# The preparation of the last attention: x in quarters, normalised on ScalarE, one half rope table, first weights split there

## The chip, the core and the metric

The kernel runs on one core of a Trainium2 chip. The metric is the device time of one execution in microseconds. A core has TensorE (PE), VectorE (DVE), ScalarE (ACT), GpSimd (POOL) and the queue of SyncE (SP), which issues all the DMAs here. The engines run beside each other and wait for each other only at semaphores.

## The reference

Four blocks follow each other on x of 32 x 64 tokens by 512, each a gated cross attention and a gated feed-forward part; every part works on the layer norm of x. The change lies ahead of the last cross attention (32 heads of 128 in 8 groups, rotary positions, 64 tokens in a sequence), cut here to what matters:

```python
x = x + tanh(g_xattn[3]) * _L3_xattn_ref(_layernorm(x), ctx, ctx, pos, mask, Wq, Wk, Wv, Wo)

q = (query @ Wq).reshape(nb, q_len, H, D).transpose(0, 2, 1, 3)
cos, sin = cos_t[position_ids][:, None], sin_t[position_ids][:, None]   # tables of 512 positions
q = q * cos + _rotate_half(q) * sin                                     # k likewise
scores = jnp.where(mask == 0, -1e9, q @ k.T / sqrt(D))
x = softmax(scores) @ v @ Wo
```

A position below zero counts from the end of the table, and positions are cut to the table's ends.

## The kernel before

The 2048 tokens are 16 tiles of 128, handled in 4 turns of 4 tiles (QUAD, TURNS). The kernel is four stages; a stage ends when all engines are done, then POOL clears each of the stage's semaphores, one by one, and all engines meet (`stage`, lines 62 to 70).

1. `prepare_weights` loads and splits the weights of the early layers into a bfloat16 high half and a low half (raw minus high). SP issues the loads in an order written out by hand; the last things are the 4 MB of Wk3 and Wv3, whose split is stored to DRAM for later.
2. `early_layers` does everything up to the last attention in four turns and stores x to DRAM (`x_mid`); it also makes all keys and values of the last attention (`k3`, `v3`).
3. `prepare_last` loads the whole x (4 MB), the positions broadcast to 128 partitions, two tables (cos and sin, [512, 128] each), the mask and the first group's Wq and Wo. VectorE turns the positions to f32, wraps and clamps them (lines 1601 to 1607, on 2048 columns). Then four turns. In a turn VectorE makes bn_stats and bn_aggr of four tiles, POOL the reciprocal root (add, power, one column at a time, lines 1560 to 1563), VectorE the normalised tile (L1626). TensorE multiplies each table with the one-hot of the turn's 512 positions (L1574; four matmuls a table, two passes each in f32) and transposes the tiles (L1581); ScalarE copies cos, sin and the high halves of the transposed tiles (L1590, L1593), VectorE their low halves (L1632). VectorE makes the one-hot of turn t + 1 (L1615) before the low halves of turn t. The mask (L1642) comes last.
4. `last_attention` runs over 8 groups (its "heads"). Before the first one ScalarE and POOL split the loaded Wq into four pieces (L1973, L2084) and Wo into four (L2001, L2098). TensorE projects the first queries (L349 to L351) piece by piece, VectorE multiplies by cos and sin (L2141 to L2143), POOL adds the two (L2079). In POOL's program the four low halves of Wo stand behind the seven first rotations and ahead of the first division by the softmax's sum (L2092). SP reloads Wo and Wq for the second group once these low halves are made.

PSUM banks are handed on by counting semaphores (`Banks`): `wait_free` waits for the last drain of a bank, `wait_filled` for its matmuls. POOL opens them with one increment for each semaphore at a stage's start.

Of the kernel before, what the change touches and what calls it, by code (L numbers as in the profile page):

```python
# [21 lines left out]
F32 = mybir.dt.float32  # L22
# [7 lines left out]
P = 128  # L30
# [44 lines left out]
def prepare_weights(nc, io, w):  # L75

    with ExitStack() as ctx:
# [16 lines left out]
        eight = sb("eight", [P, E01])  # L94
# [14 lines left out]
        def _(sp):  # L109
# [97 lines left out]
        def _(dve):  # L207
            dve.memset(w["L1W"][:, 0:3, :], 0.0).then_inc(zeroed, 1)
            dve.memset(w["heads"][:, :], 0.0).then_inc(zeroed, 1)
            for k, name in enumerate(RAW):  # L210
                dve.wait_ge(raw_high, k + 1)
                dve.tensor_tensor(w[name + "l"][:, :, :], raw[name][:, :, :], w[name + "h"][:, :, :], ALU.subtract)
# [1292 lines left out]
def prepare_last(nc, io, w):  # L1505
# [3 lines left out]
    for j in range(QUAD):  # L1509
        plan.append((("turn", j), j))  # L1510
    plan += [(("cos",), 4), (("sin",), 5)]
    with ExitStack() as ctx:
# [3 lines left out]
        def signal(name, per_turn, by=1):  # L1516
            return Signal(nc, w, "pl_" + name, per_turn, by)

        xn = sb("xn", [P, QUAD, D])
        stats, mv = sb("stats", [P, QUAD, 6]), sb("mv", [P, QUAD, 2])  # L1520
        vare, rstd = sb("vare", [P, QUAD]), sb("rstd", [P, QUAD])
        mask_raw = sb("mask", [P, TILES, SEQ], I32)
        pos_raw, pos = sb("pos_raw", [P, TOKENS], I32), sb("pos", [P, TOKENS])
        wrap = sb("wrap", [P, TOKENS])
        row = sb("row", [P, C])
        one_hot = sb("one_hot", [P, C, QUAD * P])
        table = sb("table", [P, 2, C, P])
        banks = Banks(nc, ctx, w, "pl", plan)
        x_loaded = new_semaphore(nc, w, "pl_x_loaded")
        pos_loaded, tables_loaded = new_semaphore(nc, w, "pl_pos_loaded"), new_semaphore(nc, w, "pl_tables_loaded")  # L1530
        mask_loaded, heads_loaded = new_semaphore(nc, w, "pl_mask_loaded"), new_semaphore(nc, w, "pl_heads_loaded")
        row_ready = new_semaphore(nc, w, "pl_row_ready")
        once = new_semaphore(nc, w, "pl_once")
        stats_ready, rstd_ready, xn_ready = signal("stats_ready", 4), signal("rstd_ready", 4), signal("xn_ready", 4)
        xT_high, hot_ready = signal("xT_high", 4), signal("hot_ready", 4)
        dve_step = new_semaphore(nc, w, "pl_dve_step")
        pool_step = new_semaphore(nc, w, "pl_pool_step")
        block = ctx.enter_context(nc.Block())
        PER = QUAD * P

        @block.sync
        def _(sp):
            sp.dma_start(pos_raw[:, :], io["pos"].partition_broadcast(P)).then_inc(pos_loaded, 16)
            sp.dma_start(table[:, 0, :, :], io["cos"].rearrange("(c p) n -> p c n", p=P)).then_inc(tables_loaded, 16)
            sp.dma_start(table[:, 1, :, :], io["sin"].rearrange("(c p) n -> p c n", p=P)).then_inc(tables_loaded, 16)
            sp.dma_start(w["X"][:, :, :], io["x_mid"].rearrange("(t p) n -> p t n", p=P)).then_inc(x_loaded, 16)
            sp.dma_start(mask_raw[:, :, :], io["mask"].rearrange("(t p) n -> p t n", p=P)).then_inc(mask_loaded, 16)
            load_q(sp, io, w, 0).then_inc(heads_loaded, 16)
            load_o(sp, io, w, 0).then_inc(heads_loaded, 16)
            sp.wait_ge(heads_loaded, 32)  # L1550

        @block.gpsimd
        def _(pool):
            banks.open(pool)
            pool.iota(row[:, :], pattern=[[P, C]], base=0, channel_multiplier=1,
                      allow_small_or_imprecise_dtypes=True).then_inc(row_ready, 1)
            with pool.Fori(0, TURNS) as turn:
                for j in range(QUAD):
                    stats_ready.wait(pool, turn, j)
                    pool.tensor_tensor(vare[:, j:j + 1], mv[:, j, 1:2], w["eps"][:, :], ALU.add)\  # L1560
                        .then_inc(pool_step, 1)
                    pool.wait_ge(pool_step, turn * QUAD + (j + 1))
                    rstd_ready.send(pool.tensor_tensor(rstd[:, j:j + 1], vare[:, j:j + 1], w["power"][:, 0:1],
                                                       ALU.pow))

        @block.tensor
        def _(pe):
            pe.wait_ge(tables_loaded, 32)
            with pe.Fori(0, TURNS) as turn:
                for k, step in enumerate(("cos", "sin")):  # L1570
                    hot_ready.wait(pe, turn, QUAD - 1)
                    banks.wait_free(pe, turn, step)
                    for c in range(C):
                        last = pe.matmul(banks.bank(step), table[:, k, c, :], one_hot[:, c, :],  # L1574
                                         start=(c == 0), stop=(c == C - 1))
                    banks.fill(last, step)
# [828 lines left out]
```

## Time and profile before

| | us |
|---|---|
| median of 3 runs | 2311.14 (2310.07 to 2311.7) |
| the profiled execution, its own time | 2309.02 |
| its span in the trace | 2307.3 |
| PE busy | 1930.9 (84%) |
| DVE busy | 1694.7 (73%) |
| POOL busy | 604.1 (26%) |
| ACT busy | 560.0 (24%) |

A busy share is a mean over stages with different limits. The profile also gives TensorE's granted clock in tenths of full speed (1.00 is 2.4 GHz, 0.50 is 1.2 GHz), the chain of work that ended last, for each group of instructions what its engine waited for, and a timeline. Times in a timeline are from the start of the span; "x4" stands for four instructions merged, with their total.

### The profile page before, as it was taken

The page shows a single profiled execution, that of the slowest core. Times are in us where ns is not written, and L with a number is a line of the kernel's source. Part 1 is how long each engine was busy: PE and PEld are TensorE (multiplying, and loading weights), DVE is VectorE, ACT ScalarE, POOL GpSimd, SP SyncE. Part 2 cuts the span into 40 slices and gives each one's busy share as a digit, 9 for nine tenths or more (in the row PEclk, how much of TensorE's full clock was granted, in tenths as well). Part 3 has the DMA queues.
Part 4 walks back from the last instruction along what each step waited for, and adds up shares of the span by engine and source line. Part 5 has one row for each costly group of instructions (what it writes and reads, how often), then busy time and mean ns, then how long its engine had stood idle before and what let it go on. Part 6 is the DMA issues. An engine that isn't in the chain of part 4 may idle for free. (4 is left out here: it accounts for less than half of the span.)

```text
span 2307.3 us, 40366 instructions
## 1 busy us (share of the span) xinstructions
PE 1930.9 (84%) x14722; PEld 1103.7 (48%) x14872; DVE 1694.7 (73%) x3005; ACT 560.0 (24%) x1326; POOL 604.1 (26%) x728
## 2 busy tenths in 40 slices
PE   4488778887788777888775789999999999999876
PEld 3344456434564345643452345555455545555432
DVE  4379754896558965489653688888888888888875
ACT  3122223212232122321221212222222222222221
POOL 0210203102131021310210354444344434343210
PEclk7699877998779987899775999999999999999987
DMA  6447201572014720157004111212111111111101
GB/s 216 146 125 215 83 1 38 137 203 82 1 46 136 198 80 1 47 133 211 14 1 136 60 56 47 65 28 74 43 50 45 55 47 46 47 28 29 33 24 37
DMA packets 134607, 176.82 MB, mean 77 GB/s; under 512 B 46304, under 2 KB 73568, under 8 KB 134288
## 3 DMA queue, kind: packets, MB, share of 16 engines
q1 hardware_dynamic: 134416, 174.20, 25.5%
q8 instruction: 129, 2.11, 0.4%
q14 instruction: 62, 0.51, 0.1%
HBM read 132.09 MB, written 42.07 MB: 75 GB/s over the span
## 5 line engine op out<-in xcount | busy, mean ns | idle before, releaser
L1138 POOL TENSOR_TENSOR early_vare<-early_mv,w_eps 128x1 f32<-128x1 f32 x96 | 31.5, 328 | 839.6 <-DVE early_mv L1203 825.0
L350 PE MATMUL la_ps<-w_xTl,la_wqh 128*128 128x512 bf16 x512 | 197.2, 385 | 16.1 <-POOL la_wql L2084 8.0
L2079 POOL TENSOR_TENSOR la_q<-la_straight,la_rot 128x512 f32<-128x512 f32 x128 | 163.3, 1276 | 168.7 <-DVE la_rot L2143 168.7
L350 PE MATMUL la_ps<-la_wol,la_oTh 128*128 128x512 bf16 x512 | 199.7, 390 | 6.7 <-issue 0.2
L351 PE MATMUL la_ps<-la_woh,la_oTl 128*128 128x512 bf16 x512 | 199.5, 390 | 0.0
L349 PE MATMUL la_ps<-w_xTh,la_wqh 128*128 128x512 bf16 x504 | 195.0, 387 | 3.9 <-DVE la_rot L2143 3.8
L351 PE MATMUL la_ps<-w_xTh,la_wql 128*128 128x512 bf16 x510 | 195.9, 384 | 0.0
L752 PE MATMUL early_ps<-early_products,w_heads 128*32 128x512 f32 x1024 | 129.6, 629 | 63.1 <-DVE early_products L1354 32.0
L2092 POOL TENSOR_TENSOR la_p<-la_s,la_rec 128x256 f32<-128x256 f32 x128 | 93.0, 727 | 324.9 <-DVE la_rec L2164 324.9
L2025 ACT ACTIVATE la_oTh<-la_ps 128x256 bf16<-128x256 f32 x256 | 84.3, 381 | 301.7 <-PE la_ps L1936 301.7
L349 PE MATMUL la_ps<-la_woh,la_oTh 128*128 128x512 bf16 x392 | 153.1, 391 | 0.0
L1354 DVE TENSOR_TENSOR early_products<-early_pR,early_vR 128x4096 f32<-128x4096 f32 x32 | 140.1, 4419 | 9.7 <-DMA early_pR<-scr_p 9.7
L1341 DVE TENSOR_TENSOR early_products<-early_qs,early_kp 128x4096 f32<-128x4096 f32 x32 | 140.0, 4418 | 0.0
L1978 ACT ACTIVATE la_s<-la_s 128x256 f32<-128x256 f32 x128 | 53.3, 417 | 356.0 <-DVE la_s L2157 356.0
L657 PE MATMUL early_ps<-w_ident,early_xn 128*128 128x128 f32 x320 | 63.3, 351 | 87.6 <-DVE early_xn L1207 86.7
L2178 DVE SCALAR_TENSOR_TENSOR w_X<-la_ps,w_gates,w_X 128x512 f32<-128x512 f32 x128 | 96.1, 751 | 30.3 <-PE la_ps L351 27.5
L2171 DVE TENSOR_TENSOR la_oTl<-la_ps,la_oTh 128x256 bf16<-128x256 f32 x256 | 96.0, 417 | 16.1 <-ACT la_oTh L2025 10.8
L657 PEld LDWEIGHTS early_ps<-w_ident,early_xn 128*128 128x128 f32 x320 | 48.3, 180 | 109.1 <-DVE early_xn L1207 99.1
L2141 DVE TENSOR_TENSOR la_straight<-la_ps,w_cos 128x512 f32<-128x512 f32 x128 | 88.3, 690 | 12.7 <-PE la_ps L351 11.2
L1895 PE MATMUL la_ps<-la_k,la_q 128*64 128x64 f32 x2048 | 88.8, 229 | 8.4 <-issue 8.4
L752 PEld LDWEIGHTS early_ps<-early_products,w_heads 128*32 128x32 f32 x1024 | 28.8, 111 | 139.2 <-issue 77.0
L2163 DVE TENSOR_REDUCE la_tot<-la_s 128x4 f32<-128x256 f32 x128 | 53.6, 419 | 55.6 <-ACT la_s L1978 55.6
(329 smaller groups left out, 4725.0 us busy)
## 6 DMA issues: line engine op xcount, KB each, us to landing
early_vR<-scr_v SPq DMA_DIRECT2D x128, 257.0 KB, 5.2
early_wkv<-wkv SPq DMA_DIRECT2D x32, 512.0 KB, 4.4
la_v<-v SPq DMA_DIRECT2D x64, 256.0 KB, 3.8
k<-early_ctxt SPq DMA_DIRECT2D x32, 256.0 KB, 3.6
v<-early_ctxt SPq DMA_DIRECT2D x64, 128.0 KB, 2.8
scr_p<-early_weights SPq DMA_DIRECT2D x16, 512.0 KB, 2.7
early_pR<-scr_p SPq DMA_DIRECT2D x32, 256.0 KB, 3.4
w_raw_q<-in_Wq SPq DMA_DIRECT2D x8, 1024.0 KB, 6.7
```

Of the source, the lines that this page charges most:

```text
L349: pe.matmul(out, lh[c], rh[c], start=(first and c == 0), stop=False)
L350: pe.matmul(out, lh[c], rl[c], start=False, stop=False)
L351: ins = pe.matmul(out, ll[c], rh[c], start=False, stop=(last and c == n - 1))
L657: last = pe.transpose(out[:, c * P:(c + 1) * P], xn[:, j, c * P:(c + 1) * P], ident)
L752: last = pe.matmul(out[32 * g:32 * g + 32, :], w["heads"][:, HEADS * (1 - odd):HEADS * (1 - odd) + 32], src(2 * g + odd), start=(opens and ...
L1341: qk_ready.send(dve.tensor_tensor(product[h][:, :, :, :], queries(j, h), keys_by_shift(j, h), ALU.mult))
L1354: pv_ready.send(dve.tensor_tensor(by_depth(j, h), pR[:, j % 2, h, :].unsqueeze(1).to_broadcast([P, CH, D]), vR[:, j % 2, :, h:h + D], ALU. ...
L1895: last = pe.matmul(out[SEQ * b:SEQ * b + SEQ, h * SEQ:(h + 1) * SEQ], q[:, m, h, cols], k[:, m, cols], start=True, stop=True, skip_group_c ...
L2079: rope_sum.send(pool.tensor_tensor(dst, straight[:, slot, :], rot[:, slot, :], ALU.add))
L2092: p_ready.send(pool.tensor_tensor(p[:, slot, :, :], s[:, slot, :, :], rec[:, slot, :].unsqueeze(2).to_broadcast([P, GROUP, SEQ]), ALU.mult))
L2171: banks.drain(dve.tensor_tensor(mine[0], banks.bank(name, n, u, *L)[:, 0:2 * P].rearrange("p (h t) -> p h t", h=2), mine[1], ALU.subtract) ...
L2178: banks.drain(dve.scalar_tensor_tensor(out=tile, in0=banks.bank("out", n, u, *L), scalar=w["gates"][:, 3:4], in1=tile, op0=ALU.mult, op1=A ...
```

## The change

In `prepare_weights` the positions are loaded as [16, 128], wrapped and clamped there on VectorE, and stored as f32 to DRAM (`pos3`). In `prepare_last` the loops are written out. x is loaded in four quarters, each with its own semaphore. POOL makes the reciprocal roots of four tiles at once, and offset = -mean x rstd; ScalarE normalises (scale and bias as columns). There is one table [512, 128] with cos in the first 64 columns and sin in the others; ScalarE copies both to partitions 0 to 63, POOL copies cos to 64 to 127 and writes -sin there. The first Wq and Wo are split here by ScalarE and POOL, and their tiles live across both stages; `last_attention` starts with them made.

```diff
@@ prepare_weights
             sp.dma_start(gates_raw[:, :], io["gates"].partition_broadcast(P)).then_inc(gates_loaded, 16)
+            sp.dma_start(pos_raw[:, :], io["pos"].rearrange("(t p) -> t p", p=P)).then_inc(pos_loaded, 16)
...
                 sp.dma_start(raw3[:, i, :, :], io[name].rearrange("(c p) n -> p c n", p=P)).then_inc(kv_loaded, 16)
+            sp.wait_ge(pos_step, 4)
+            sp.dma_start(io["pos3"].rearrange("(t p) -> t p", p=P), pos[:, :]).then_inc(pos_kept, 16)
+            sp.wait_ge(pos_kept, 16)
...
+            dve.wait_ge(pos_loaded, 16)
+            dve.tensor_copy(pos[:, :], pos_raw[:, :]).then_inc(pos_step, 1)
+            dve.wait_ge(pos_step, 1)
+            dve.tensor_scalar(below[:, :], pos[:, :], 0.0, float(POSITIONS), ALU.is_lt, ALU.mult).then_inc(pos_step, 1)
...
@@ prepare_last, SP
+            load_x(0)
+            pos_loaded.send(sp.dma_start(pos[:, :], io["pos3"].partition_broadcast(P)))
+            table_loaded.send(sp.dma_start(table[:, :, :], io["rope"].rearrange("(c p) n -> p c n", p=P)))
+            load_x(1)
+            load_x(2)
+            q_loaded.send(load_q(sp, io, w, 0))
+            load_x(3)
+            o_loaded.send(load_o(sp, io, w, 0))
+            mask_loaded.send(sp.dma_start(mask_raw[:, :, :], io["mask"].rearrange("(t p) n -> p t n", p=P)))
@@ prepare_last, POOL
+            def rstd_of(t):
+                pool.wait_ge(stats_ready.sem, t + 1)
+                moments.send(pool.tensor_tensor(vare[:, quad(t)], mv[:, quad(t), 1],
+                                                w["eps"][:, :].to_broadcast([P, QUAD]), ALU.add))
...
+                rstd_ready.send(pool.tensor_tensor(rstd[:, quad(t)], vare[:, quad(t)],
+                                                   w["power"][:, 0:1].to_broadcast([P, QUAD]), ALU.pow))
...
+                offset_ready.send(pool.tensor_tensor(offset[:, quad(t)], mv[:, quad(t), 0], rstd[:, quad(t)],
+                                                     ALU.mult))
+            def double(t):
+                pool.wait_ge(half_ready.sem, 2 * t + 2)
+                pool.wait_ge(offset_ready.sem, min(t + 3, TURNS))
+                doubled.send(pool.tensor_copy(w["cos"][64:128, tokens(t)], w["cos"][0:64, tokens(t)]))
+                pool.wait_ge(doubled.sem, 2 * t + 1)
+                doubled.send(pool.tensor_scalar(w["sin"][64:128, tokens(t)], w["sin"][0:64, tokens(t)], -1.0, None,
+                                                ALU.mult))
...
+            rstd_of(0); rstd_of(1); rstd_of(2); double(0); rstd_of(3); low_q(0); low_q(1); ...
+            double(1); low_q(2); low_q(3); ...; double(2); low_o(0..3); ...; double(3)
@@ prepare_last, PE
+            for t in range(TURNS):
+                rope(t)        # waits for hot(t): 4 matmuls of the one table
+                turn_x(t)      # waits for the normalised tiles: 16 transposes
@@ prepare_last, ACT
+            normalise(0); normalise(1); high(0); half_rope(0); normalise(2); high_q(0); high_q(1)
+            high(1); half_rope(1); normalise(3); high_q(2); high_q(3)
+            high(2); half_rope(2); high_o(0..3); high(3); half_rope(3)
@@ prepare_last, DVE
+            statistics(0); hot(0); statistics(1); low(0); statistics(2); hot(1); low(1)
+            statistics(3); hot(2); low(2); hot(3); mask; low(3)
@@ last_attention
         def _(sp):
             sp.sem_inc(o_loaded.sem, 16)
+            for split in (q_high, q_low, o_high, o_low):
+                sp.sem_inc(split.sem, GROUP)
...
                 if which is not None:
-                    q_low.wait(pe, 0, PIECES.index(f"q{which}"))
                     project_q(0, place, step, which)
...
-            for piece in PIECES:
-                high_of(piece)
-            o_loaded.wait(act, 0, 0)
-            for h in range(GROUP):
-                high_o(0, h)
             exponentials(0, 0, 0)
...
-            for piece in PIECES:
-                low_of(0, 0, piece)
             for i, (place, which, step) in enumerate(FIRST):
                 add_rotation(0, place, i % 2, rotated(which, step))
-            for h in range(GROUP):
-                low_o(0, 0, h)
             divide(0, 0, 0)
```

The orders of calls are drawn together into few lines here. `statistics` is bn_stats and bn_aggr of a quarter's four tiles and a negation of the means; `hot` the one-hot of a turn; `low` and `high` the halves of its four transposed tiles; `half_rope` ScalarE's two copies of the table's product.

## Rows read from the trace of the kernel before

**Rows 1.** The page's slices, 57.7 us each: TensorE's busy tenths.
```profile
PE   4488778887788777888775789999999999999876
```
**Rows 2.** SP's waits, 1238 to 1345: us, times, longest.
```profile
SPq L72 <- PEq L72: 7.4, 2, 5.4
```
**Rows 3.** Timeline: start us, us, engine, line, operation, [idle before <-releaser]; stage's start.
```profile
1248.57 0.35 SPq L1543 DMA_DIRECT2D pl_pos_raw<-in_pos  x1
...
1266.47 2.47 DVE L1620 BATCH_NORM_STATS2 pl_stats<-w_X 128x6 f32 x4 [5.25 <-DMA w_X<-x_mid]
...
1268.86 0.37 DVE L1623 BATCH_NORM_AGGREGATE pl_mv<-pl_stats 128x2 f32<-128x6 f32 x4
...
1269.37 0.55 POOL L1563 TENSOR_TENSOR pl_rstd<-pl_vare,w_power 128x1 f32<-128x1 f32 x1
```
**Rows 4.** Timeline of the preparation's third turn.
```profile
1284.27 1.67 DVE L1615 TENSOR_SCALAR pl_one_hot<-pl_pos,pl_row 128x512 f32 x4
...
1285.86 2.48 DVE L1632 TENSOR_TENSOR w_xTl<-pl_ps,w_xTh 128x512 f32 x4
...
1286.08 7.13 PE L1574 MATMUL pl_ps<-pl_one_hot,pl_table 128*128 128x512 f32 x16 [1.01 <-DVE pl_one_hot L1615]
...
1293.04 1.04 PE L1581 MATMUL pl_ps<-w_ident,pl_xn 128*128 128x128 f32 x8
```
**Rows 5.** Timeline of the preparation's end.
```profile
1305.62 1.91 PE L1581 MATMUL pl_ps<-w_ident,pl_xn 128*128 128x128 f32 x16
...
1306.39 2.06 ACT L1593 ACTIVATE w_xTh<-pl_ps 128x512 f32 x4
1307.02 2.48 DVE L1632 TENSOR_TENSOR w_xTl<-pl_ps,w_xTh 128x512 bf16<-128x512 f32 x4 [0.90 <-ACT w_xTh L1593]
1309.42 0.68 DVE L1642 TENSOR_SCALAR w_mask<-pl_mask 128x1024 bf16<-128x1024 int32 x1
```
**Rows 6.** DMA issues, 1240 to 1330: KB each, median us to landing.
```profile
w_X<-x_mid SPq DMA_DIRECT2D x1, 4096.0 KB, 16.2
```
**Rows 7.** Timeline of the last attention's start.
```profile
1312.48 2.19 ACT L1973 ACTIVATE la_wqh<-w_raw_q 128x512 bf16<-128x512 f32 x4 [4.02 <-PEq L72]
...
1315.48 0.63 PE L350 MATMUL la_ps<-w_xTl,la_wqh 128*128 128x512 bf16 x1 [7.95 <-POOL la_wql L2084]
...
1339.36 0.18 DVE L2164 RECIPROCAL la_rec<-la_tot 128x4 f32<-128x4 f32 x1
...
1342.91 2.08 POOL L2092 TENSOR_TENSOR la_p<-la_s,la_rec 128x256 f32<-128x256 f32 x2
...
1353.55 0.75 DVE L2178 SCALAR_TENSOR_TENSOR w_X<-la_ps,w_gates,w_X 128x512 f32<-128x512 f32 x1 [0.65 <-PE la_ps L351]
```
**Rows 8.** The chain of waits, same stretch: start us, us, what.
```profile
1312.28 0.06 issue
...
1350.97 0.38 PE la_ps L350
```
**Rows 9.** Stretches: their us, PE busy us (instructions), granted clock, DMA share, GB/s.
```profile
1307.60:1310.60 3.00, 0.00 (x0) 1.00 0.00 0
...
1315.50:1317.70 2.20, 2.20 (x6) 0.50 0.92 243
...
1344.00:1348.50 4.50, 4.00 (x29) 0.50 0.91 313
...
1261.40:1266.40 5.00, 5.00 (x6) 0.50 1.09 361
```
**Rows 10.** Groups of the whole span: busy us, mean ns | idle before.
```profile
L1147 POOL TENSOR_TENSOR early_xq<-early_xq,w_gbias 128x512 f32<-128x512 f32 x48 | 60.9, 1301 | 0.0
...
L1150 POOL MEMSET early_vp<- 128x1056 f32 x1 | 1.0, 992 | 0.0
...
L998 ACT ACTIVATE early_kp<-early_ps,w_L1b 128x512 f32<-128x512 f32 x16 | 11.0, 685 | 2.0 <-PE early_ps L745 1.9
```
**Rows 11.** Timeline of stage one: ScalarE splits the last 4 MB loaded.
```profile
43.61 7.68 ACT L202 ACTIVATE prep_split<-prep_raw 128x1024 bf16<-128x1024 f32 x8 [6.80 <-DMA prep_raw<-in_Wv]
```

More of the change, by code:

```diff
@@ L1530, in prepare_last @@
[L1530 to L1535, printed above, removed]
@@ L1541, in _, with tokens @@
+        def tokens(t):
+            return slice(t * PER, (t + 1) * PER)
         @block.sync
         def _(sp):
[L1543 to L1546, printed above, removed]
@@ L1554, in _ @@
             banks.open(pool)
[L1555 to L1564, printed above, removed]
+            row_ready.send(pool.iota(row[:, :], pattern=[[P, C]], base=0, channel_multiplier=1,
+                                     allow_small_or_imprecise_dtypes=True))
@@ L1569, in _ @@
[L1569 to L1572, printed above, removed]
-                    for c in range(C):
-                        last = pe.matmul(banks.bank(step), table[:, k, c, :], one_hot[:, c, :],
-                                         start=(c == 0), stop=(c == C - 1))
-                    banks.fill(last, step)
-                for j in range(QUAD):
-                    xn_ready.wait(pe, turn, j)
-                    banks.wait_free(pe, turn, "turn", j)
-                    for c in range(C):
-                        last = pe.transpose(banks.bank("turn", j)[:, c * P:(c + 1) * P],
-                                            xn[:, j, c * P:(c + 1) * P], w["ident"][:, :])
-                    banks.fill(last, "turn", j)
+            pe.wait_ge(table_loaded.sem, 16)
@@ new lines, in rope, with turn_x @@
+            def rope(t):
+                pe.wait_ge(hot_ready.sem, t + 1)
+                banks.wait_free(pe, 0, "rope", t)
+                for c in range(C):
+                    last = pe.matmul(banks.bank("rope", t), table[:, c, :], one_hot[:, c, :],
+                                     start=(c == 0), stop=(c == C - 1))
+                banks.fill(last, "rope", t)
+            def turn_x(t):
+                for j in range(QUAD):
+                    pe.wait_ge(xn_ready.sem, t * QUAD + j + 1)
+                    banks.wait_free(pe, 0, "turn", t, j)
+                    for c in range(C):
+                        last = pe.transpose(banks.bank("turn", t, j)[:, c * P:(c + 1) * P],
+                                            xn[:, t % 2, j, c * P:(c + 1) * P], w["ident"][:, :])
+                    banks.fill(last, "turn", t, j)
@@ L1614, in hot @@
+            def hot(t):
+                if t >= 1:
+                    banks.wait_filled(dve, 0, "rope", t - 1)
                 for c in range(C):
-                    hot_ready.send(dve.tensor_scalar(one_hot[:, c, :], pos[:, bass.ts(turn, PER)],
-                                                     row[:, c:c + 1], None, ALU.is_equal))
-            def body(turn, more):
+                    last = dve.tensor_scalar(one_hot[:, c, :], pos[:, tokens(t)], row[:, c:c + 1], None, ALU.is_equal)
+                hot_ready.send(last)
@@ L1628, in body @@
-                if more:
-                    hot(turn + 1)
-                for j in range(QUAD):
-                    xT_high.wait(dve, turn, j)
-                    banks.drain(dve.tensor_tensor(w["xTl"][:, :, bass.ts(turn * QUAD + j, P)],
-                                                  banks.bank("turn", j).rearrange("p (c n) -> p c n", c=C),
-                                                  w["xTh"][:, :, bass.ts(turn * QUAD + j, P)], ALU.subtract),
-                                "turn", j)
```

209 lines of the change are left out of this document (150 added, 59 removed).

## The prediction

> **What bounds the kernel now.** I read the page's slices first [rows 1]. The digits before the 22nd slice are the four repetitions of the early layers, which the change leaves alone but for one small table; from the 24th slice TensorE is at 8 or 9 tenths and sets the pace. The 22nd and 23rd slices (57.7 us each) hold what the change touches: the end of the early layers, the preparation, and the start of the last attention. Then the timeline of that stretch, in order: the stage's loads are issued from 1248.57 and its last instruction, the mask on VectorE, ends at 1310.10, so the preparation lasts 61.5 us [rows 3 to 5]. Its first 17.9 us wait for data: VectorE handles the positions in the meantime, but its statistics start at 1266.47, when all of x has landed. Then three turns of 10.9 us and a last one of 13.1. A turn at full clock is TensorE's 16 rope passes (1286.08 to 1293.04, 6.96 us, 0.435 each), the four tiles' transposes, ScalarE's high halves, then VectorE's low halves; the one-hot table of the next turn is built before the low halves, so the next passes start (1286.08) while these are still running [rows 4]. Last the next stage, its timeline and the chain of waits [rows 7, 8]: POOL opens the banks one increment at a time from 1312.28, is then held for the first low half of the first weights until 1315.04, and TensorE starts at 1315.48. Further on the chain passes through 4.8 us of POOL's low halves of Wo, and only behind them does POOL make its first division, at 1342.91.
>
> **The preparation after the change.** Times here are from the stage's start (1248.57). I follow the one chain that ends last.
> - Data. One MB takes 2.9 us: 5.5 MB had landed 17.7 us after the start, 2 of them latency [rows 6]. The new order is x quarter 0 (1 MB), positions (1), the table (0.25), quarter 1 (1). Quarter 0 lands at about 4.9, the positions at 7.8, quarter 1 at 11.3. Quarter 2, first Wq, quarter 3, first Wo and the mask follow until 25, ahead of their uses. VectorE's four position operations leave this stage; they lay in the wait for x.
> - Statistics of a quarter: 2.76 us from 1266.47 to the end of the aggregates [rows 3], and a negation with its waits, about 0.4: 3.15. POOL: add 0.19, power over four columns, multiply 0.2 with waits. A one-column power took 0.55 [rows 3]; four columns lie between that and four times it (2.2). I take 1.0, nearer to the single row, since the operation has a fixed part: 1.6 in all. ScalarE's normalisation has no row with two column operands. With one it took 0.685 [rows 10], some 0.09 more than a copy; four splits of that size took 2.19 us, one every 0.55 [rows 7]. Two operands make that 0.72 each, four tiles 2.9 (bounds 2.2 and 3.3).
> - The start: quarter 1 at 11.3, statistics 3.15, POOL 1.6, normalisation of quarter 1 2.9 (ScalarE does it before the high halves of quarter 0). High to low 0.63 and four low halves 2.48 [rows 5]: the low halves of quarter 0 end at 22.05. The first rope passes (from about 10, half clock) and transposes are done by 18 and hide.
> - The cycle. VectorE's order is now low halves (t), statistics (t+2), one-hot (t+1), and TensorE takes rope (t+1) before the transposes (t+1), which the low halves (t+1) need. Nothing overlaps: statistics 3.15, one-hot 1.67 and 0.14 until TensorE starts [rows 4], rope R, then 0.77 to the first high half and 3.11 to the end of the low halves [rows 5]. That is 8.9 + R.
> - R. One table instead of two: 8 passes, 3.48 us at full clock. But TensorE now idles about 8 us and 7 us ahead of rope 1 and 2. In this trace the granted clock stood at its lower level (1.2 GHz, 0.50) after such pauses: after 8 us without a matmul it stayed there 2.3 us into the work, after 4.4 us 4.5 us into it, and in the first rope passes 5.1 us, six passes in 5.0 us [rows 9]. I take the mean, 3.9 us, which costs half of itself: R is 5.4. Ahead of rope 3 it idles 3.5 us; I take 4.9. Bounds: 3.48 (all at 2.4 GHz) and 6.8 (8 passes by 0.85).
> - Two whole cycles of 14.3 end at 50.6. The last: one-hot 1.67 + 0.14 + 4.9 = 57.3. Then ScalarE's high halves, 0.77 + 2.06, the two halves of the rope table 1.2, and POOL's doubling: copy and negation of 64x512. Nearest rows [rows 10]: a memset of 1056 columns 0.99, an addition of 512 columns 1.30; so 0.5 to 1.3 each, I take 0.9, 1.8 and 0.15 of waits. End: 63.3, against 61.5: **+1.8**.
> - ScalarE and POOL beside it: POOL has rstd of quarter 3 in front of the splits of Wq and frees at about 57; ScalarE's high halves of Wo end at 53. Both lie under the chain. If a split of 1.15 us on POOL came late, the stage's end would move by what is left of it.
>
> **Semaphores.** At a stage's end SP waits for POOL's clears: 7.4 us for the early layers (69) and this stage (26) together, 5.4 of it the former, and 1.8 for the first stage (23) [rows 2]: 0.078 each. Here there are 12 more, 0.94; in the first stage 3 more, 0.23. **+1.2.**
>
> **The positions in stage one.** One load of 8 KB more, four tiny VectorE operations, one store. The load goes ahead of the weights' on SP's queue (0.4 us of issue); the later weight loads are followed by transfers until 43.6, where ScalarE waits for the last of 4 MB [rows 11], while SP had issued them by 29.4, so the issue is hidden. VectorE waits for the positions before its first split; they are issued ahead of that split's weights, so they land first. The store is issued about 30, and SP then waits for it until at most 45, with only waits behind it and the weights' store due at 56.8. Zero, at most 0.5.
>
> **The last attention.** TensorE no longer waits for the split; its bank is open 0.16 us into the stage, and 0.3 to 0.45 pass to the first matmul, so 1312.75 for 1315.48: **-2.7**. What is late next is VectorE's key rotation, 5.8 us after the first matmul; its 256 KB are issued at the stage's opening, and a whole MB takes 4.9, so it holds. Wo's low halves leave the chain: the reciprocal was ready at 1339.54 and POOL divided at 1342.91 [rows 7]: 3.4 us. Next are TensorE's projection until 1339.6 and the transposes about 1340.7. VectorE is full there (two rotations until 1347.7), but the first output projection, which went at 1350.97 [rows 8], waits for the low halves behind them, about 1347.5, and the work in front of it no longer begins at half clock. I keep **-3.4** (bounds: 0.7, the only gap VectorE showed until 1353.55 [rows 7], and 4.8, all of the splits). The earlier reloads of Wo and Wq (2 MB, about 1324 for 1343) find the queue empty.
>
> A page speaks against the new order: the Trainium skill, TensorE: Matmul & The Clock Gate, section HAM oscillation, has a matmul loop whose waits between bursts put the array back to half clock, so that every burst starts cold; by it R is the 5.4 above, without it 3.48 and the sum 5.2 us lower (the first rival). The trace agrees at 1344.03 and 1315.48.
>
> **Sum.** +1.8 + 1.2 - 2.7 - 3.4 = -3.1. Against the profiled execution (span 2307.3, time 2309.02) that is 2305.9; the median of the runs, 2311.14, is 2.1 above that execution, so I forecast **2308.0**. A change under 0.2% (4.6 us: 2306.5 to 2315.8) can't be told from none.
>
> **Rivals.**
> 1. TensorE keeps full clock between turns. For it: the granted clock stood at 1.00 for the 3 us after the matmuls had ended at 1307.6 [rows 9]. Against: it was down when the next ones came. R is 3.48 three times: -1.9 - 1.9 - 1.4, so 2302.8. Chance 0.2.
> 2. VectorE hides what POOL gives back: only 0.7 of the 3.4 counts. For it: VectorE's unbroken row from 1334.7 to 1352.9. Against: TensorE waits there for the low halves behind the rotations, and these have 3.4 us of room. 2310.7. Chance 0.14.
> 3. Slower: TensorE stays at half clock through every rope block. It decides where the clock's rise comes later than 6.8 us into a block: R is 6.8 three times (+1.4 + 1.4 + 1.9), the transposes double (0.3 a turn), and the next stage's first twelve matmuls take 5.1 for 3.6: +1.5. 2308.0 + 7.1 = 2315.1, 4.0 above the median of before. For it: each cycle has fewer columns than now; against: the rise within 5.1 us each time. Chance 0.12.
> 4. The stage does what its parts promise, and the serial order costs nothing because VectorE does without the normalisations (8.7 us) and half the rope is gone: it would end near 50, and the time be 2295. For it: that work does go. Against: the order of the code, low halves before one-hot before rope. Chance 0.04.
>
> **Numbers.** The forecast case has 0.5, with 2304.5 to 2311.5 of its own. Range 2302.5 to 2313.5: both bounds of R in part, the unknown POOL durations. Faster by over 0.2%: rivals 1 and 4 and a quarter of the forecast case, 0.36. Slower by over 0.2%: the upper half of rival 3 with what I overlook, 0.09. Within: 0.55.
>
> **What would show it.** In the new trace: first statistics near 5 and not 18 us into the stage; TensorE idle 7 to 8 us ahead of rope 1 and 2 with the granted clock at 0.50 when they start; a cycle of 13 to 15 us from one rope block to the next; the mask or POOL's last doubling 61 to 66 us in; TensorE's first matmul under 0.6 us after the stage opens; the first division right behind its reciprocal. A stage under 58 us, or a clock of 1.00 at the start of rope 1, makes the forecast wrong.

## The result, and the profile after

The changed kernel takes 2301.5 us (median of 6 runs, 2299.26 to 2303.72); the kernel before, beside it on the same chip, 2311.42 (6 runs, 2309.1 to 2317.69). The ratio is 0.9948, 95% interval 0.9933 to 0.9963: some 12 us or 0.5% less, where 3.1 less was forecast, and outside the range. The profiled execution took 2301.86 us, its span is 2300.1 (2307.3 before).

The table sets each step's forecast against the two traces. "Third addition" is the third tile added to X by the last attention (the third start of `w_X<-la_ps,w_gates,w_X`, of 128); the times are differences between starts in the two traces.

| | forecast | measured |
|---|---|---|
| preparation, opening to last operation | 61.5 to 63.3 | 61.53 to 65.57 |
| preparation's opening to TensorE's first matmul of the last attention | 66.9, unchanged | 66.91 to 69.08 |
| first matmul to third addition | -3.4 | 51.60 to 48.91: -2.7 |
| preparation's opening to third addition, in all | -3.4 | 118.52 to 117.99: -0.5 |
| 3rd to 47th addition, 51st to 79th, 83rd to 128th | none | 297.93, 189.59, 362.2: all as before |
| **47th to 51st addition** | none | 34.58 to 29.04: **-5.5** |
| **79th to 83rd addition** | none | 33.04 to 28.90: **-4.1** |

The preparation opened 2.9 us later in this trace, which is no effect of the change: over all the traces taken for this study it opened between 1245.1 and 1258.1, for the same early code. With it the differences add up to the 7.2 us of the spans. The stretch up to the third addition varies too where no edit touches it: in three more traces of kernels with the old stage it took 118.42, 118.60 and 120.91 us (padded by 12, 24 and 121 instructions, below), in two more of the changed stage 118.15 and 118.01. So the -0.5 of this pair stands for something between -0.3 and -2.9.

So the rewritten stage and the moved splits together gave little, half a microsecond in this pair, and the rest came from two short places in the middle of the last attention, in code that the diff does not touch. I asked both traces what TensorE waits for from 1640 to 1900, where these places lie. Before:

```profile
PE la_ps L1895 <- issue: 8.4, 4, 3.4
```

After (columns: line waited for, us in total, times, longest):

```profile
PE la_ps L2014 <- issue: 2.3, 2, 1.5
```

"issue" says that no semaphore held TensorE: it had nothing to run. Four such stops became two. The timeline of before shows the first pair (columns as in [rows 3]):

```profile
1664.91 0.72 PE L1936 MATMUL la_ps<-la_pT,la_v 64*128 64x128 f32 x8
1666.67 0.44 PE L1895 MATMUL la_ps<-la_k,la_q 128*64 128x64 f32 x7 [1.04 <-issue]
1670.52 0.79 PE L1895 MATMUL la_ps<-la_k,la_q 128*64 128x64 f32 x9 [3.41 <-issue]
1671.24 0.61 PE L349 MATMUL la_ps<-w_xTh,la_wqh 128*128 128x512 bf16 x1
1671.64 0.63 PE L350 MATMUL la_ps<-w_xTl,la_wqh 128*128 128x512 bf16 x1
```

and the same place after:

```profile
1667.30 0.72 PE L2055 MATMUL la_ps<-la_pT,la_v 64*128 64x128 f32 x8
1669.50 0.69 PE L2014 MATMUL la_ps<-la_k,la_q 128*64 128x64 f32 x16 [1.48 <-issue]
1670.12 0.39 PE L363 MATMUL la_ps<-w_xTh,w_wqh 128*128 128x512 bf16 x1
```

This is where the last attention's loop over pairs of heads (three pairs, so two backward branches) goes back to its head. Before, the sixteen score matmuls of one unit are cut in the middle by a second stop of 3.41 us, and the matmuls behind it follow one another by 0.43 us for 0.22. Stretches of 5 us around it show the clock (columns as in [rows 9], with VectorE, ScalarE and POOL in between). Before:

```profile
1665.00:1670.00 5.00, 1.07 (x15) 0.74 (x15) 1.51 (x3) 0.66 (x2) 0.84 (x1) 0.94 0.45 111
1670.00:1675.00 5.00, 4.48 (x18) 1.95 (x19) 3.04 (x7) 0.42 (x1) 1.10 (x1) 0.50 0.66 213
```

After:

```profile
1665.00:1670.00 5.00, 3.52 (x35) 1.92 (x33) 2.62 (x4) 0.86 (x3) 1.77 (x2) 1.00 0.12 37
1670.00:1675.00 5.00, 5.00 (x31) 2.47 (x27) 3.86 (x9) 0.80 (x2) 1.10 (x1) 1.00 0.91 277
```

The second stop also brings the granted clock to its lower level. That is the 5.5 us: 3.0 less of standing (4.45 before, 1.48 after), and twelve matmuls of the projection by 0.43 instead of 0.215, 2.6.

TensorE's branch itself took 3.53 us in the trace before (at 1662.97) and 3.94 us in the trace after (at 1665.40); its queue of matmuls covers most of that. The page's third part has the queue that brings instructions, 16 KB a time; after:

```profile
q8 instruction: 129, 2.11, 0.4%
```

```profile
q8 instruction: 1, 0.02, 3.1%
```

Rivals: the moved splits or the freed engines removed the stop.

The stage itself, TensorE after:

```profile
1261.99 5.71 PE L1641 MATMUL pl_ps<-pl_one_hot,pl_table 128*128 128x512 f32 x8 [21.87 <-DVE pl_one_hot L1733]
1267.54 1.91 PE L1650 MATMUL pl_ps<-w_ident,pl_xn 128*128 128x128 f32 x16
1278.36 6.08 PE L1641 MATMUL pl_ps<-pl_one_hot,pl_table 128*128 128x512 f32 x8 [8.90 <-DVE pl_one_hot L1733]
1284.27 1.91 PE L1650 MATMUL pl_ps<-w_ident,pl_xn 128*128 128x128 f32 x16
1292.76 5.70 PE L1641 MATMUL pl_ps<-pl_one_hot,pl_table 128*128 128x512 f32 x8 [6.58 <-DVE pl_one_hot L1733]
1298.30 1.91 PE L1650 MATMUL pl_ps<-w_ident,pl_xn 128*128 128x128 f32 x16
1304.40 6.71 PE L1641 MATMUL pl_ps<-pl_one_hot,pl_table 128*128 128x512 f32 x8 [4.18 <-DVE pl_one_hot L1733]
```

TensorE stands 8.9, 6.6 and 4.2 us ahead of each block, and eight passes take 5.7 to 6.7 us where the clock stays at full they take 3.70. Its start and end, on the other engines:

```profile
1251.49 0.40 SPq L1565 DMA_DIRECT2D w_X<-x_mid  x1
...
1257.04 2.47 DVE L1718 BATCH_NORM_STATS2 pl_stats<-w_X 128x6 f32<-128x512 f32 x4 [13.78 <-DMA w_X<-x_mid]
...
1260.42 1.17 POOL L1589 TENSOR_TENSOR pl_rstd<-pl_vare,w_power 128x4 f32<-128x4 f32 x1
...
1314.88 0.61 POOL L1598 COPY w_cos<-w_cos 64x512 f32<-64x512 f32 x1 [5.19 <-issue]
1315.58 1.48 POOL L1600 TENSOR_SCALAR w_sin<-w_sin 64x512 f32<-64x512 f32 x1
...
1320.57 0.61 PE L363 MATMUL la_ps<-w_xTh,w_wqh 128*128 128x512 bf16 x1 [7.72 <-POOLq L292]
```

The first statistics come 5.6 us into the stage (17.9 before, [rows 3]), and the last doubling ends 65.6 us in. In the last attention the first division now stands right behind its reciprocal, where [rows 7] had 3.4 us between the two, taken up by the weights' low halves:

```profile
1345.19 0.18 DVE L2273 RECIPROCAL la_rec<-la_tot 128x4 f32<-128x4 f32 x1
...
1345.45 0.61 POOL L2205 TENSOR_TENSOR la_p<-la_s,la_rec 128x256 f32<-128x256 f32 x1 [1.48 <-DVE la_rec L2273]
```

And SP's waits for the clears, the row of [rows 2], after: 0.8 more, 0.94 forecast for this stage.

```profile
SPq L72 <- PEq L72: 8.2, 2, 5.4
```

### The profile page after: what moved, and what is told of

It reads as the page before. It is cut to its first block and busy times, and to the rows that moved or that the text cites. A ratio compares the mean times of both kernels' runs of the same rounds, so it can differ in the third digit from the quotient of the medians.

```text
span 2300.1 us, 40311 instructions
## 1 busy us (share of the span) xinstructions
PE 1927.6 (84%) x14840; PEld 1095.8 (48%) x14840; DVE 1679.0 (73%) x2993; ACT 570.8 (25%) x1342; POOL 604.9 (26%) x716
## 5 line engine op out<-in xcount | busy, mean ns | idle before, releaser
L363 PE MATMUL la_ps<-w_xTh,w_wqh 128*128 128x512 bf16 x512 | 197.3, 385 | 18.0 <-DVE la_rot L2252 10.3
L363 PE MATMUL la_ps<-w_woh,la_oTh 128*128 128x512 bf16 x512 | 199.5, 390 | 1.0 <-DVE la_oTl L2280 0.7
L364 PE MATMUL la_ps<-w_wol,la_oTh 128*128 128x512 bf16 x512 | 199.9, 390 | 0.0
L365 PE MATMUL la_ps<-w_woh,la_oTl 128*128 128x512 bf16 x512 | 198.9, 389 | 0.0
L364 PE MATMUL la_ps<-w_xTl,w_wqh 128*128 128x512 bf16 x512 | 195.9, 383 | 0.0
L365 PE MATMUL la_ps<-w_xTh,w_wql 128*128 128x512 bf16 x512 | 195.4, 382 | 0.0
L2287 DVE SCALAR_TENSOR_TENSOR w_X<-la_ps,w_gates,w_X 128x512 f32<-128x512 f32 x128 | 96.1, 751 | 27.6 <-PE la_ps L365 24.5
L2055 PEld LDWEIGHTS la_ps<-la_pT,la_v 64*128 64x128 f32 x1024 | 67.9, 186 | 53.4 <-issue 51.2
```

The costliest lines, as they stand in the source:

```text
L363: pe.matmul(out, lh[c], rh[c], start=(first and c == 0), stop=False)
L364: pe.matmul(out, lh[c], rl[c], start=False, stop=False)
L365: ins = pe.matmul(out, ll[c], rh[c], start=False, stop=(last and c == n - 1))
L2055: last = pe.matmul(out[:, :, cols], v2[rows, m, u, b, :], pT[rows, u % 2, :, cols], start=True, stop=True)
L2287: banks.drain(dve.scalar_tensor_tensor(out=tile, in0=banks.bank("out", n, u, *L), scalar=w["gates"][:, 3:4], in1=tile, op0=ALU.mult, op1=A ...
```

## The experiments

Each ratio is to the kernel before, run beside it on the same chip, with its 95% interval. A padding of n waits becomes n/2 instructions of TensorE, ahead of the preparation's first rope block: they wait on a semaphore that has its value, and cost time only where TensorE would be late (0.11 us each). The kernel before had medians of 2311.4 to 2315.1 us on the chips used, so ratios are to be compared, not the times of different chips.

### Is it the place of the code?

Before, padded by 121 instructions (as many as the change adds):

```
+            for _ in range(242):
+                pe.wait_ge(banks.drained[0], 1)
             pe.wait_ge(tables_loaded, 32)
```

> The kernel before, with 121 extra TensorE instructions (waits that are already satisfied) ahead of the first rope block, where TensorE idles for 12 us. Nothing else changes; TensorE's loop over the pairs of groups now begins at the same place within a 16 KB instruction load as in the changed kernel. Theory L (layout): the 9.7 us that the changed kernel gains inside the last attention come from where its loop begins: in the kernel before, TensorE stops 3.4 us a few instructions behind the loop's branch at 1667 and at 1891 and then works at half clock for a while. With the padding those two stops go, the preparation stays as it is (61 to 62 us), and the time falls by 8 to 10 us to 2301 to 2303. Theory W (work): the gain comes from the weights' earlier loads and splits; then the padding changes nothing, 2311 within 2.

Measured: 2300.14 us (2298.49 to 2303.62), ratio 0.993 (0.9917 to 0.9942). The preparation stayed at 61.72 us; 47th to 51st addition 28.99, 79th to 83rd 28.90. Instructions that do nothing gave the whole of the change's gain. The loop stretches give 9.7 us, as expected; the ratio says 13 to 19 us, more than that and more than the 8 to 10 expected, and what the rest is stays open: in this trace the stretch up to the third addition was 2.4 us longer, not shorter.

The changed kernel, padded by 135 instructions (`range(270)`, ahead of its wait for the table), so that by the count the loop's head is back at its old place within a line:

> The changed kernel with 135 extra TensorE instructions ahead of its first rope block, so that the pair loop begins where it does in the kernel before. Theory L: the stops of 3.4 us behind the loop's branch come back and the time rises by 8 to 10 us from the changed kernel's 2301.5, to 2310 to 2311, about the kernel before: the change itself is then worth nearly nothing. Theory W: stays at 2301.5 within 2.

Measured: 2313.32 us (2306.31 to 2317.51, 11 runs), ratio 0.9993 (0.9982 to 1.0003). Stops of 3.47 and 2.89 us are back, the two stretches take 34.98 and 32.83. The cut lies behind the third of the sixteen scores, where it lay behind the seventh before; each score is two instructions, so the head is 9 ahead of the line here and not 17, and 144 in the changed kernel and not 152, which changes nothing in the argument. The preparation took 65.68 us, so the padding cost it nothing. At equal layout the change is worth 1.6 us, between 4.2 less and 0.7 more.

Two that lie on either side of the line: before, padded by 12 instructions (`range(24)`: 5 ahead of the line) and by 24 (`range(48)`: 7 behind it, so 249 ahead of the next).

> The kernel before, with 12 more TensorE instructions (24 waits that are always satisfied) in the last attention's preparation. In the compiled program the pair loop's first instruction is now 5 instructions ahead of the next 16 KB line of TensorE's code, where it was 17 ahead. Rival N (the number of instructions, or anything added ahead of the loop, shakes the stops off): 29 and 28.9, 9 to 12 us less. Preparation unchanged.

> The same with 24 instructions: the loop's first instruction now lies 7 instructions behind the line, 249 ahead of the next one. Theory L: both second stops are gone (46th to 50th addition 29.0, 78th to 82nd 28.9), 8 to 12 us less than before, by only 12 instructions more than the kernel beside it, which keeps them. Rival N: as the kernel with 12. Rival T (what takes the stops away is that whole loops behind it shift by about half a line or more, as with 121 instructions): the stops stay.

Measured: 2312.48 us, ratio 1.0003 (0.9986 to 1.002), and 2302.05 us, ratio 0.9955 (0.9939 to 0.9971). TensorE's waits from 1640 to 1910, with 12:

```profile
PE la_ps L1897 <- issue: 13.0, 4, 4.2
```

with 24:

```profile
PE la_ps L1897 <- issue: 2.4, 2, 1.3
```

With 12 the two stretches take 35.73 and 35.99, with 24 they take 28.94 and 29.06: the stops with 12 (3.64 and 4.19 us) are longer than expected for the second branch. The timeline with 12:

```profile
1671.72 0.27 PE L1897 MATMUL la_ps<-la_k,la_q 128*64 128x64 f32 x1 [2.59 <-issue]
1675.62 1.12 PE L1897 MATMUL la_ps<-la_k,la_q 128*64 128x64 f32 x15 [3.64 <-issue]
```

The cut in the sixteen scores moved from behind the seventh to behind the first: each is a weight load and a matmul, so 12 instructions earlier is 6 scores, which is what was added. Twelve more instructions and the cut is gone. The stop is tied to a place in the code. A rival by number of instructions falls, and so does one by half a line.

How far ahead is far enough? Before, padded by 193 (`range(386)`: 80 ahead of the line) and by 223 (`range(446)`: 50 ahead).

> The kernel before with 193 more TensorE instructions ahead of its loop: the pair loop's head now lies 80 instructions ahead of the next line, between the 17 that gave a second stop of 3 to 4 us and the 154 that gave none. 
> The same with 223 instructions: 50 ahead of the line. Theory L with overlap: those 50 are about 1.7 us of scores, so a shorter second stop, of 1 to 2 us, and 46th to 50th addition 30 to 32.5, between the two levels (29.0 and 34.6 to 35.7). Rival L2: one of the two levels, not between.

Measured: 2309.35 us, ratio 0.9972 (0.9957 to 0.9987), and 2318.78 us, ratio 1.0017 (0.9998 to 1.0036). With 80 the two stretches take 29.14 and 28.90: no second stop. With 50 they take 30.59 and 32.49, the first between the two levels, and the stop comes behind sixteen scores and seven projections (46 instructions of weights and matmuls), and is shorter:

```profile
1681.60 0.38 PE L349 MATMUL la_ps<-w_xTh,la_wqh 128*128 128x512 bf16 x1
1684.11 0.39 PE L350 MATMUL la_ps<-w_xTl,la_wqh 128*128 128x512 bf16 x1 [2.13 <-issue]
```

The whole times carry a cost of the padding that I had not allowed for: the instructions run from the stage's opening, 223 of them for 223 x 0.11 = 24.5 us, so the first rope block began 24.8 us in (12.8 before), and the preparation grew to 67.05 and 70.36 us. 5.5 and 8.8 more there with 9.6 and 4.5 less in the loop make 4.1 less and 4.3 more, within both intervals (121 instructions, 13.3 us, had just fitted).

### What are the parts worth?

Before, with only the splits of the first Wq and Wo moved into its preparation, and 4 instructions of padding (head 19 ahead of the line, so the stops stay):

```
+                q_high.send(act.activation(w["wqh"][:, :, bass.ts(turn, HD)], w["raw_q"][:, :, bass.ts(turn, HD)],
+                                           ACT.Copy))
...
+                pool.tensor_tensor(w["wol"][:, 0, bass.ds(turn, 1), :], w["raw_o"][:, bass.ds(turn, 1), :],
+                                   w["woh"][:, 0, bass.ds(turn, 1), :], ALU.subtract)
```

> The kernel before, with only the splits of the first Wq and Wo moved into its preparation: ScalarE and POOL make one piece of each in every turn, behind their turn's work; the pair loop keeps its place (within two instructions) by a few extra waits, so the stops at the branch stay. By the terms of the forecast this part alone is -2.7 (first matmul) -3.4 (first division) + 0.2 (two semaphores more): -5.9, 2305 to 2306. If VectorE hides the division, -3.2: 2308. If the added work of ScalarE and POOL lengthens a turn, it is dearer: ScalarE has 7 us free in a turn of 10.9 and needs 1.2.

Measured: 2309.7 us, ratio 0.9984 (0.9972 to 0.9996). Preparation 62.46, first matmul 65.49 us in (66.91 before), first matmul to third addition 48.87. In all 4.15 us less up to the third addition. The stops stayed (3.95 and 2.57 us, the first behind the eighth score, as two instructions more would have it). The ratio is 3.7 us less, 0.9 to 6.5; 5.9 was expected, and the first matmul came 1.4 us earlier and not 2.7, because POOL's added work ended the preparation 0.9 later. And the same with 125 instructions of padding:

> The kernel before with only the first weights' splits moved into the preparation (as in the third experiment), and 121 more TensorE instructions, so that its pair loop lies 154 instructions ahead of the next line. If the layout's gain (10 us) and the split's gain (4 us) are independent and add up: 14 us less than before, 2 to 6 us less than the changed kernel; stage opening to third addition 114 to 116. If they share a cause (both had moved a stop): 10 us less, no better than the changed kernel.

Measured: 2300.47 us, ratio 0.9943 (0.9925 to 0.9961), opening to third addition 114.70, loop stretches 29.14 and 29.10. By the trace the two gains add up (3.8 and 9.4 us); the ratio (13.2 us, 9 to 17) includes the 14 of the sum and does not exclude the changed kernel's.

The changed kernel with Wo's low halves put back into the last attention (layout unchanged):

```
-            for h in range(GROUP):
-                low_o(h)
-            pool.wait_ge(o_low.sem, GROUP)
             double(3)
...
+            for h in range(GROUP):
+                low_o(0, 0, h)
             divide(0, 0, 0)
```

> The changed kernel with one part undone: the low halves of the first output weights (GpSimd, 4 x 1.1 us) are subtracted in the last attention again, ahead of the first division, not in the preparation. Layout of TensorE's code unchanged. The forecast's term says that this costs 3.4 us in the last attention (first matmul to third addition 52 instead of 48.9), and gives back in the preparation what GpSimd's end is shortened by: 0 to 4.5 us (last operation 61 to 65.6 us in). Together between 1 us less and 3.5 us more than the changed kernel; if moving it was worth nothing in the sum, within 1 us.

and beside it the changed kernel once more:

> The changed kernel unaltered, so that the two kernels beside it have it on the same chip. 9 to 13 us less than before; preparation 65.6 us, stage opening to third addition 118.0.

Measured: 2305.68 us (ratio 0.9957, 0.994 to 0.9973) against 2301.69 (0.994, 0.9924 to 0.9955). First matmul to third addition 52.65 against 48.95, preparation 65.84 against 65.69. The term is 3.7 us, and costs the preparation nothing; the medians differ by 4.0, where at most 3.5 was expected.

### What makes the rewritten stage slow?

TensorE kept at work in its pauses, by transposes into a bank that nobody reads:

```
             for t in range(TURNS):
                 rope(t)
                 turn_x(t)
+                for _ in range((64, 46, 28, 0)[t]):
+                    pe.transpose(banks.ps[:, 7, 0:P], w["ident"][:, :], w["ident"][:, :])
```

> The changed kernel with 64, 46 and 28 extra transposes of the identity matrix into an unused PSUM bank behind TensorE's turns 0, 1 and 2 (nobody reads them; 105 mod 256 is where the pair loop's head comes to lie, so its layout stays good). They fill TensorE's pauses ahead of the rope blocks 1, 2 and 3 with work of about 7.5, 5.5 and 3.4 us at the full clock. Theory H (the half clock behind a pause is what makes these rope blocks 5.7 to 6.7 us where they take 3.7 at the full clock, and each lies on the serial path): blocks of 3.7 to 4.2 us, each cycle 1.5 to 2.5 us shorter, preparation 59 to 62 us, 3 to 6 us less than the changed kernel. Rival S (ScalarE and GpSimd end the cycle anyway, or the filler delays the block by what the clock gives): preparation 64 to 67, within 1.5 us of the changed kernel.

Measured: 2295.58 us, ratio 0.991 (0.9894 to 0.9926), 6.1 less than the changed kernel beside it. Preparation 60.03 us. TensorE:

```profile
1280.00 5.40 PE L1643 MATMUL pl_ps<-pl_one_hot,pl_table 128*128 128x512 f32 x8 [2.40 <-DVE pl_one_hot L1737]
...
1293.72 3.70 PE L1643 MATMUL pl_ps<-pl_one_hot,pl_table 128*128 128x512 f32 x8 [1.56 <-DVE pl_one_hot L1737]
...
1303.53 3.70 PE L1643 MATMUL pl_ps<-pl_one_hot,pl_table 128*128 128x512 f32 x8 [1.30 <-DVE pl_one_hot L1737]
```

Two blocks came down to 3.70; the first still had a pause of 2.40 ahead of it and gained 0.7. Work of no use made the kernel faster, because the block is on the serial path and its clock depends on what TensorE did before it. The length of the last pause alone does not set it: the block behind 2.40 us began at full clock, which fell 0.4 us into it (0.68 granted over the block), and in the reordered kernel below a block behind a pause of 3.38 us ran at 1.00 and took 3.70. The Trainium skill, TensorE: Matmul & The Clock Gate, section HAM oscillation, has bursts between waits start cold; the trace agrees, with 6.08, 5.70 and 6.71 us behind pauses of 4.2 to 8.9 and 3.70 behind pauses of 1.3 and 1.6; the 3.70 behind 3.38 is a burst that did not start cold.

VectorE's order, first only the one-hot tables ahead of the low halves:

```
             statistics(1)
-            low(0)
-            statistics(2)
             hot(1)
-            low(1)
-            statistics(3)
+            low(0)
+            statistics(2)
             hot(2)
-            low(2)
+            low(1)
+            statistics(3)
             hot(3)
+            low(2)
```

> The changed kernel with one edit in VectorE's order: the one-hot of turn t+1 stands ahead of the low halves of turn t, as in the kernel before. TensorE's program and its place are unchanged. If the serial order (low halves, statistics, one-hot, rope, transposes, low halves) is what keeps the changed preparation at 65.6 us, this takes it apart: rope t+1 runs while the low halves and statistics are made, and by the same terms the stage ends at about 44 to 50 us, so the time falls by 15 to 21 us to 2281 to 2287. If the half clock or a transfer keeps it, less than 5.

Measured: 2291.24 us (2288.16 to 2293.97), ratio 0.9893 (0.9879 to 0.9907). Preparation 55.60 us where 44 to 50 was expected, and 10 us less than the changed kernel where 15 to 21 was: VectorE then stood 4.7 and 5.0 us for ScalarE's high halves of turns 1 and 2, with the next statistics queued behind them. So each quarter's statistics one step earlier (`statistics(1) hot(1) statistics(2) low(0) hot(2) statistics(3) low(1) hot(3) low(2)`):

> The changed kernel with VectorE's order: statistics 0, positions compared 0, statistics 1, compared 1, statistics 2, low halves 0, compared 2, statistics 3, low halves 1, compared 3, low halves 2, mask, low halves 3: each quarter's statistics one turn earlier than in the reordered kernel, whose preparation took 55.6 us. Theory O (serial order of VectorE, GpSimd and ScalarE sets the cycle: the statistics wait behind low halves that wait for the normalisation of the turn before): preparation 45 to 50 us, then bound by GpSimd, which has some 20 us to do behind the third quarter; 5 to 10 us less than the reordered kernel, so 15 to 22 less than the changed one. Rival X (x's quarters arrive too late for it): 52 to 56 us.

Measured: 2281.58 us (2278.1 to 2288.94), ratio 0.9866 (0.984 to 0.9893), the fastest of all: some 31 us less than before, 20 less than the changed kernel. Preparation 47.1 us, opening to third addition 100.39. Its blocks:

```profile
1264.94 3.70 PE L1641 MATMUL pl_ps<-pl_one_hot,pl_table 128*128 128x512 f32 x8
...
1272.76 3.70 PE L1641 MATMUL pl_ps<-pl_one_hot,pl_table 128*128 128x512 f32 x8 [1.61 <-DVE pl_one_hot L1733]
...
1281.60 5.40 PE L1641 MATMUL pl_ps<-pl_one_hot,pl_table 128*128 128x512 f32 x8 [2.63 <-DVE pl_one_hot L1733]
```

## Why the prediction was wrong

**The step that failed** is an assumption under the sum, not a term in it: "from the 24th slice TensorE is at 8 or 9 tenths and sets the pace", and nothing behind the third addition was given a price. The changed kernel has 121 more instructions of TensorE ahead of the pair loop, which moves the loop's head from 17 to some 150 instructions ahead of a line of code, and two second stops with the half clock behind them went: -9.7 us in the traces. Padding alone gives it to the kernel before, padding back takes it from the changed one, and 12 instructions decide it. The row stood in the trace: four stops put down to "issue" inside a full TensorE, 8.4 us, which a slice of the page hides: 4 us of standing in 57.7 still read as 9 tenths (and the last two slices are at 7 and 6, which the prediction passed over). The Trainium skill, Advanced Engine Details and Errata, section ISA Cache, has lines of 16 KB, 256 instructions; the loads of this trace agree (129 loads of 16 KB), and so does the place of the cut. The Trainium skill, Advanced Engine Details and Errata, section Control Flow Timing, gives a compare-and-branch some 108 ns; by it such a loop costs next to nothing. In the preparation's own short loop (L1569 of the kernel before) TensorE's branch back took 0.21 to 0.24 us, but 3.3 to 4.9 us in the pair loop, where its target had to be loaded.

**The sum that I did make**, -3.1, stands at equal layout at -1.6 (-4.2 to +0.7). By its steps:
- The data's arrival, the order of the work and the length of the cycle came out right, the cycle partly by luck: one-hot tables 1 to 3 began 25.1, 39.5 and 50.5 us in, worked out 25.2, 39.5 and 50.6; the power over four columns took 1.0 to 1.17, taken 1.0; four normalisations 2.93, taken 2.9. But rope blocks 1 and 2 took 6.08 and 5.70 us where R was 5.4, and the steps from their ends to the next one-hot tables 6.6 and 3.5 where the terms give 7.0 and 3.9, which made up for it. Rival 1 (full clock between turns) is out by the pauses' clock, and rival 3 (half clock throughout, 6.8 a block) came true for the last block alone.
- The last turn was mis-sized, and it is all of the 2.3 us by which the stage missed: its one-hot table took 2.37 us beside POOL's work (1.67 alone), and its rope block 6.71 where I took 4.9, having read from the shorter pause that the clock would rise sooner. The rise came later, 6.1 us into the block, at a granted clock of 0.55 over the block. The tail behind it took 6.0 as forecast, though POOL's negation (1.48 us) lay above its bound of 1.3.

```profile
1304.40:1311.10 6.70, 6.70 (x10) 2.82 (x11) 0.95 (x1) 0.00 (x0) 5.21 (x5) 0.55 0.00 0
```

- The first matmul of the last attention: from the stage's last operation it came 3.5 us later, 5.4 before; +0.9 -2.7 were the terms, so right.
- Wo's low halves: -3.4 forecast, 3.7 by the experiment that puts them back. The stretch in the two traces shows only -2.7, but in five more traces of kernels that keep both splits in the last attention it took 52.0 to 53.8 us, and in two more of the changed kernel, one of them padded, 48.4 and 49.0, so that pair lies at the small end of -2.7 to -5.4. Rival 2 (only 0.7 of it counts) is out.
- Stage one's 0.2 to 0.7 can't be told: the early layers' first memset starts at 71.97 (72.47 before), and between 71.5 and 73.5 in the traces of kernels that share that code.

**Rival 4** is out by its condition, that the serial order costs nothing: it costs 10 us of preparation, which one swap gives back (65.6 to 55.6), and 8.5 more with the second. Its price for a stage without that order, "near 50", was about right: it came to 47.1.

## What to carry to other kernels

- Ask a full engine's stretch for its "issue" waits before you price a change. A loop that is entered once per backward branch pays for loading its head's code, and a second time when the head lies within some tens of instructions ahead of the next 16 KB line; any edit ahead of it in the program moves that place. Compare two versions at equal layout (padding gives it), or the layout's 10 us pass for the edit's.
- In a chain of engines, hoist what the next turn needs (statistics, one-hot) ahead of what only the end needs (low halves): two swaps of lines on VectorE were worth 20 us, against 12 for the whole change and 1.6 for what it did at equal layout.
- A short block on the serial path should find TensorE at work: eight passes cost 3.70 or up to 6.71 us here, by what TensorE did before them.

## What was not expected of the hardware

- A backward branch of TensorE took 3.3 to 4.9 us here, the following line of code up to 4.2 more, by the distance: 2.6 to 4.2 us of standing with 5 to 19 instructions in between, 2.13 and 2.40 with 50, none with 80. Between 5 and 19 no order shows, and the course from 50 to 80 is not shown.
- A wait that is already satisfied is not free in hundreds: 0.11 us for each instruction of two.
- VectorE slows beside POOL: four comparisons of 128x512 took 1.67 us alone and 2.37 to 3.43 beside POOL's copies, negations and subtractions (ScalarE's normalisations beside them left 1.67 in the fastest kernel). That POOL's were the cause was read from the timelines, and not tried by itself.
